# A spline evaluated on two engines: the far product and one sum move from VectorE and a transfer to GpSimd

## The reference

```python
x_aff = clip(x * a[c] + b[c], -1.5, 1.5)
u = (x_aff + 1.0) * 0.5 * (K - 1)              # K = 32 knots
i = floor(u); t = clip(u - i, 0, 1)
spline = sum(alpha_table[i + n - 1] * basis_n(t) for n in range(4))     # indices clipped, R = 8 columns
y_nl = einsum('bchwr,cr->bchw', spline, mix)
return id_gain[c] * x + y_nl + bias[c]
```

## Time and profile before

| | |
|---|---|
| time, median of 3 runs | 1149.39 us (1149.33 to 1150.38) |
| span of the profiled execution | 1143.4 us |
| between the two | 6.0 us, ahead of the first and behind the last instruction |
| PE busy | 1088.0 us, 95% of the span |
| DVE busy | 969.9 us, 85% |
| ACT busy | 898.8 us, 79% |
| POOL busy | 138.8 us, 12% |
| mean granted TensorE clock | 0.991 |

### The profile page before, as it was taken

The page is one execution under the profiler, slowest core; times in us unless marked ns, Lnnn a source line. Parts: engine busy times, 40 slices in busy tenths (PEclk is TensorE's granted clock), DMA queues, the critical chain, the costliest instruction groups (busy, mean ns, idle before and its releaser), DMA issues.

```text
span 1143.4 us, 51639 instructions
## 1 busy us (share of the span) xinstructions
PE 1088.0 (95%) x23882; PEld 726.6 (64%) x23882; DVE 969.9 (85%) x959; ACT 898.8 (79%) x410; POOL 138.8 (12%) x195
## 2 busy tenths in 40 slices
PE   6999999699999959999999999999999999999996
PEld 5777777577777735666666656565665666566564
DVE  4856656687767679999999999999998999999997
ACT  4445453766777548999999999999999999999971
POOL 6000000068100000110101101011010110110100
PEclk9999999899999989999999999999999999999999
DMA  8677674677676937799999999989999989999652
GB/s 278 227 293 283 251 283 175 220 257 301 248 296 270 373 137 173 183 235 232 221 228 218 222 236 216 224 201 236 226 214 231 218 217 235 219 226 209 150 127 86
DMA packets 57459, 259.37 MB, mean 227 GB/s; under 512 B 16080, under 2 KB 16080, under 8 KB 49232
## 3 DMA queue, kind: packets, MB, share of 16 engines
q1 hardware_dynamic: 48496, 208.40, 56.0%
q0 software_dynamic: 8640, 48.17, 23.1%
q10 hardware_dynamic: 160, 0.30, 0.1%
HBM read 104.29 MB, written 77.07 MB: 159 GB/s over the span
## 4 chain that ended last, share of the span: by engine, by line
PE 86%; DVE 7%; issue 3%; DMA 1%; ACT 1%; SPq 0%; ACTq 0%; DVEq 0%
PE tab L1302 48%; PE acc L741 30%; PE tab L1311 7%; DMA halo<-y_scratch 1%; DMA w_raw<-in_w 1%; DVE middle_mask L1160 1%; ACT xin L381 1%; ACT yout L420 1%; DVE far L1187 0%; DVE far_sq L1209 0%; DVE stats L547 0%; DVE lin L1139 0%; DVE offset L1153 0%; DVE edge_mask L1169 0%; DVE poly L1215 0%
## 5 line engine op out<-in xcount | busy, mean ns | idle before, releaser
L1302 PE MATMUL tab<-edge_mask,diag 128*32 128x392 bf16 x10240 | 447.6, 329 | 6.1 <-issue 3.2
L1302 PEld LDWEIGHTS tab<-edge_mask,diag 128*32 128x32 f16 x10240 | 277.0, 97 | 171.0 <-issue 29.4
L1057 ACT ACTIVATE edge_mask<-cell,thr 128x6272 bf16<-128x6272 bf16 x62 | 338.6, 5508 | 1.7 <-DMA cell<-cell 1.7
L420 ACT ACTIVATE yout<-acc 128x1568 f32<-128x1568 f32 x64 | 94.5, 1477 | 167.2 <-PE acc L741 146.3
L741 PE MATMUL acc<-band_split,w 64*64 64x385 f16 (+2 forms) x4608 | 194.8, 329 | 9.8 <-DVE band_split L509 4.5
L741 PE MATMUL acc<-split,w 64*64 64x385 f16 (+3 forms) x4608 | 191.5, 326 | 11.5 <-DVE w L468 10.5
L547 DVE BATCH_NORM_STATS2 stats<-yout 128x392 f32 (+1 forms) x240 | 117.9, 555 | 88.8 <-ACT yout L420 88.8
L1302 PE MATMUL tab<-middle_mask,diag 128*32 128x392 bf16 x4096 | 185.1, 329 | 6.7 <-issue 4.5
L741 PEld LDWEIGHTS acc<-band_split,w 64*64 64x64 f16 x4608 | 148.3, 109 | 56.1 <-issue 8.8
L741 PEld LDWEIGHTS acc<-split,w 64*64 64x64 f16 x4608 | 144.8, 108 | 57.5 <-issue 12.2
L1302 PEld LDWEIGHTS tab<-middle_mask,diag 128*32 128x32 f16 x4096 | 109.2, 97 | 70.3 <-issue 7.7
(11 more groups left out here) (140 smaller groups left out, 961.6 us busy)
## 6 DMA issues: line engine op xcount, KB each, us to landing
y_scratch<-yout SPq DMA_DIRECT2D x32, 1568.0 KB, 6.1
cell<-cell SPq DMA_DIRECT2D x496, 98.0 KB, 5.1
xin<-y_scratch SPq DMA_DIRECT2D x16, 1568.0 KB, 6.2
lin<-far POOLq DMA_DIRECT2D x32, 784.0 KB, 9.4
out<-lin SPq DMA_DIRECT2D x31, 784.0 KB, 5.8
xin<-in_x SPq DMA_DIRECT2D x15, 1568.0 KB, 6.8
lin<-y_scratch SPq DMA_DIRECT2D x30, 784.0 KB, 9.3
lin<-in_x POOLq DMA_DIRECT2D x28, 784.0 KB, 8.1
```

Of the source, the lines that this page charges most:

```text
L420: act.activation(yout[b][:, :].rearrange("p (r k x) -> p k r x", r=2, k=TILES)[:, 2 * part:2 * part + 2], acc[:, 4 * part:4 * part + 4, 0: ...
L1057: act.activation(mask_of(c, q)[:, :, :], cell4[c % 2][:, :, :], ACT.Sign, bias=thr[:, q:q + 1]).then_inc(sign_mask_ready, 1)
L1302: mm = pe.matmul(tab[(c + t) % 2][j * GROUP:(j + 1) * GROUP, sub, 0:SUB], keep["diag"][part][:, j % 2, t, q, :], mask_of(c, q)[:, j, sub * ...
```

## The change

VectorE's `far_part` and GpSimd's `add_far` go. GpSimd gets two tensor operations per chunk instead, each over 128 x 1568 fp32 elements with two SBUF inputs: `far_part` (`far` times `far_sq`, without the amplitude) and `add_terms` (`far` plus `poly`). VectorE's `slope` writes in place over `offset`, read as fp32 (`sloped`). `slope_and_far` takes the place of `add_slope` and adds the far product to the slope term, in `far`. `value` then adds the value term to `far`. GpSimd's `add_terms` adds the square term, which is left in `poly`, and `finish` multiplies this sum by the amplitude and adds it to `lin`. `finish` now waits for `add_terms`, and `slope_and_far` for GpSimd's `far_part`. For the last chunk VectorE makes the sum itself (`last_terms`).

```diff
         copied = [sem(f"cell_copied{b}") for b in range(2)]
         stored = [sem(f"out_stored{b}") for b in range(LIN)]
         x_added = sem("x_added")
-        far_added = sem("far_part_added")
         scaled = sem("scaled")
         sum_ready = sem("sum_ready")
         sum_half = sem("first_half_sum_ready")
...
         table_used = sem("table_used")
         far_part_ready = sem("far_part_ready")
         dist_sq_ready = sem("dist_sq_ready")
-        slope_ready = sem("slope_ready")
+        slope_ready = sem("slope_and_far_ready")
+        terms_added = sem("terms_added")
         whole = sem("chunk_whole")
         block = keep["block"]
...
         def used(c, t):
             return TABLES * c + t + 1
+
+        def sloped(c):
+
+            return offset[c % 2][:, :].bitcast(F32)
         def image_half(t, c):
             return t[c // 2][:, (c % 2) * CHUNK:(c % 2 + 1) * CHUNK]
...
                 pool.wait_ge(scaled, c - AHEAD + 1)
                 pool.dma_start(lin_of(c)[:, :], image_half(x, c), accum_op=ALU.add).then_inc(x_added, 16)
-            def add_far(c):
-
-                pool.wait_ge(far_part_ready, c + 1)
-                pool.dma_start(lin_of(c)[:, :], far[c % 2][:, :], accum_op=ALU.add).then_inc(far_added, 16)
+            def far_part(c):
+
+                pool.wait_ge(table_used, used(c, T_FAR))
+                pool.wait_ge(far_sq_ready, c + 1)
+                pool.tensor_tensor(far[c % 2][:, :], far[c % 2][:, :], far_sq[:, :],
+                                   ALU.mult).then_inc(far_part_ready, 1)
+
+            def add_terms(c):
+
+                pool.wait_ge(table_used, used(c, T_VAL))
+                pool.tensor_tensor(far[c % 2][:, :], far[c % 2][:, :], poly[c % 2][:, :],
+                                   ALU.add).then_inc(terms_added, 1)
             for c in range(CHUNKS):
                 if AHEAD <= c + 3 < CHUNKS:
                     add_x(c + 3)
-                add_far(c)
+                far_part(c)
+                if c < CHUNKS - 1:
+                    add_terms(c)
         @block.scalar
         def _(act):
...
             def distance(c):
                 act.wait_ge(offset_ready, c + 1)
+                wait_past(act, terms_added, c - 1)
+                act.activation(poly[c % 2][:, :], offset[c % 2][:, :], ACT.Abs, scale=1 / POINT).then_inc(dist_ready, 1)
+
+            def far_distance(c):
+
+                act.wait_ge(dist_ready, c + 1)
                 wait_past(act, whole, c - 1)
-                act.activation(poly[c % 2][:, :], offset[c % 2][:, :], ACT.Abs, scale=1 / POINT).then_inc(dist_ready, 1)
-
-            def far_distance(c):
-
-                act.wait_ge(dist_ready, c + 1)
-                wait_past(act, far_added, 16 * (c - 1))
                 act.activation(far[c % 2][:, :], poly[c % 2][:, :], ACT.Relu, bias=cc(MINUS_1)).then_inc(far_ready, 1)
             def far_square(c):
                 act.wait_ge(far_ready, c + 1)
-                wait_past(act, slope_ready, c)
+                wait_past(act, far_part_ready, c)
                 act.activation(far_sq[:, :], far[c % 2][:, :], ACT.Square).then_inc(far_sq_ready, 1)
             def distance_square(c):
...
                 dve.scalar_tensor_tensor(out=quarters(far[c % 2]), in0=summed(c, T_FAR), scalar=base(c, T_FAR),
                                          in1=quarters(far[c % 2]), op0=ALU.add, op1=ALU.mult).then_inc(table_used, 1)
-            def far_part(c):
-
-                dve.wait_ge(table_used, used(c, T_FAR))
-                dve.wait_ge(lin_ready, c + 1)
-                dve.scalar_tensor_tensor(out=far[c % 2][:, :], in0=far[c % 2][:, :], scalar=cc(AMP), in1=far_sq[:, :],
-                                         op0=ALU.mult, op1=ALU.mult).then_inc(far_part_ready, 1)
-
             def square(c):
                 dve.wait_ge(dist_sq_ready, c + 1)
...
             def slope(c):
+                dve.wait_ge(dist_ready, c + 1)
+                dve.wait_ge(dist_sq_ready, c + 1)
+                dve.wait_ge(table_ready, used(c, T_LIN))
+                dve.scalar_tensor_tensor(out=quarters(sloped(c)), in0=summed(c, T_LIN), scalar=base(c, T_LIN),
+                                         in1=quarters(offset[c % 2]), op0=ALU.add, op1=ALU.mult).then_inc(table_used, 1)
+
+            def slope_and_far(c):
+
+                dve.wait_ge(table_used, used(c, T_LIN))
                 dve.wait_ge(far_part_ready, c + 1)
-                dve.wait_ge(table_ready, used(c, T_LIN))
-                dve.scalar_tensor_tensor(out=quarters(far_sq), in0=summed(c, T_LIN), scalar=base(c, T_LIN),
-                                         in1=quarters(offset[c % 2]), op0=ALU.add, op1=ALU.mult).then_inc(table_used, 1)
-
-            def add_slope(c):
-
-                dve.wait_ge(table_used, used(c, T_LIN))
-                dve.scalar_tensor_tensor(out=poly[c % 2][:, :], in0=far_sq[:, :], scalar=1 / POINT,
-                                         in1=poly[c % 2][:, :], op0=ALU.mult, op1=ALU.add).then_inc(slope_ready, 1)
+                dve.scalar_tensor_tensor(out=far[c % 2][:, :], in0=sloped(c), scalar=1 / POINT,
+                                         in1=far[c % 2][:, :], op0=ALU.mult, op1=ALU.add).then_inc(slope_ready, 1)
             def value(c):
                 dve.wait_ge(slope_ready, c + 1)
                 dve.wait_ge(table_ready, used(c, T_VAL))
-                dve.scalar_tensor_tensor(out=quarters(poly[c % 2]), in0=summed(c, T_VAL), scalar=base(c, T_VAL),
-                                         in1=quarters(poly[c % 2]), op0=ALU.add, op1=ALU.add).then_inc(table_used, 1)
+                dve.scalar_tensor_tensor(out=quarters(far[c % 2]), in0=summed(c, T_VAL), scalar=base(c, T_VAL),
+                                         in1=quarters(far[c % 2]), op0=ALU.add, op1=ALU.add).then_inc(table_used, 1)
             def finish(c):
-                dve.wait_ge(table_used, used(c, T_VAL))
-                dve.wait_ge(far_added, 16 * (c + 1))
-                dve.scalar_tensor_tensor(out=lin_of(c)[:, :], in0=poly[c % 2][:, :], scalar=cc(AMP),
+                dve.wait_ge(terms_added, c + 1)
+                dve.wait_ge(lin_ready, c + 1)
+                dve.scalar_tensor_tensor(out=lin_of(c)[:, :], in0=far[c % 2][:, :], scalar=cc(AMP),
                                          in1=lin_of(c)[:, :], op0=ALU.mult, op1=ALU.add).then_inc(whole, 1)
-            def closing_quarters():
+            def last_terms():
                 c = CHUNKS - 1
                 dve.wait_ge(slope_ready, CHUNKS)
-                dve.wait_ge(far_added, 16 * CHUNKS)
+                dve.wait_ge(table_used, used(c, T_SQ))
+                dve.tensor_tensor(poly[c % 2][:, :], poly[c % 2][:, :], far[c % 2][:, :],
+                                  ALU.add).then_inc(terms_added, 1)
+
+            def closing_quarters():
+
+                c = CHUNKS - 1
+                dve.wait_ge(terms_added, CHUNKS)
+                dve.wait_ge(lin_ready, CHUNKS)
                 for sub in range(4):
                     own = slice(sub * SUB, (sub + 1) * SUB)
                     dve.wait_ge(table_ready, used(c, T_VAL) + sub)
...
             total(3)
             far_cube(0)
             linear(0)
-            far_part(0)
             middle(1, MIDDLE_QUADS[0])
             square(0)
             offsets(1)
             slope(0)
             middle(1, MIDDLE_QUADS[1])
-            add_slope(0)
+            slope_and_far(0)
             value(0)
             linear(1)
             linear(2)
...
                 near_cube(c)
                 finish(c - 1)
                 far_cube(c)
-                far_part(c)
                 if c + 1 < CHUNKS:
                     middle(c + 1, MIDDLE_QUADS[0])
                 square(c)
...
                 slope(c)
                 if c + 1 < CHUNKS:
                     middle(c + 1, MIDDLE_QUADS[1])
-                add_slope(c)
+                slope_and_far(c)
+            last_terms()
             closing_quarters()
         @block.tensor
```

More of the change, by code:

```diff
@@ L1030, in distance @@
                 act.wait_ge(offset_ready, c + 1)
-                wait_past(act, whole, c - 1)
+                wait_past(act, terms_added, c - 1)
                 act.activation(poly[c % 2][:, :], offset[c % 2][:, :], ACT.Abs, scale=1 / POINT).then_inc(dist_ready, 1)
@@ L1036, in far_distance @@
                 act.wait_ge(dist_ready, c + 1)
-                wait_past(act, far_added, 16 * (c - 1))
+                wait_past(act, whole, c - 1)
                 act.activation(far[c % 2][:, :], poly[c % 2][:, :], ACT.Relu, bias=cc(MINUS_1)).then_inc(far_ready, 1)
@@ L1221, in value @@
                 dve.wait_ge(table_ready, used(c, T_VAL))
-                dve.scalar_tensor_tensor(out=quarters(poly[c % 2]), in0=summed(c, T_VAL), scalar=base(c, T_VAL),
-                                         in1=quarters(poly[c % 2]), op0=ALU.add, op1=ALU.add).then_inc(table_used, 1)
```

(18 more changed lines are left out.)

## The result

The changed kernel takes 1199.16 us (median; 1197.56 to 1200.41), against 1149.89 us for the kernel before in the same rounds: a ratio of 1.042, 95% interval 1.039 to 1.045. The change is a loss of about 50 us. The forecast was 1186 us and slower, with a range of 1147 to 1206 and, for its likeliest case, 1168 to 1206.

The account below looks back on a forecast made before the run. PE bounds the kernel before at 21.99 us a chunk, DVE the changed one at 23.03. Span 1143.4 plus 28 (27 chunks), 4 (first two), 1.85 (end), with 6.0 around it and 3 for signals: 1186 us, range 1147 to 1206.

Parts of the forecast that it names:

- DVE becomes the bound: Per chunk, DVE's 19.15 us of work plus both stalls gives 23.03 us, above PE's 21.99.
- The two engines exclude each other, both ways and for a whole operation: POOL operations and DVE's `fixed`, `linear`, `offsets`, `middle` block each other; faint sign: a small DVE step 46 ns longer.
- The price of an operation: Each POOL tensor operation of 1568 elements takes 3.55 us, range 3.3 to 3.85.
- The second stall, at `finish`: `add_terms` on POOL starts behind `linear`, so DVE's `finish` waits 1.97 us for it each chunk.
- the rival given 0.07: POOL gets in between `fixed` and `linear`; `linear` stands 3.65 us, `finish` not: 24.7 us a chunk, 1229 us; chance 0.07.
- The first stall, at `offsets`: POOL's `far_part` starts behind the first `middle` and runs beside `square`; DVE's `offsets` then stands for 1.91 us.
- The sum: 19.15 us of DVE work plus stalls of 1.91 and 1.97 makes 23.03 us a chunk; 1186 us in all.
- The 3 us for signal delays at the hand-overs: Two hand-overs from POOL each chunk, 0.05 us each, would add 3 us in all.
- The end: After the last chunk, `last_terms` adds a two-tensor step on DVE, 1.85 us.
- What the transfers are worth: Removing the `add_far` transfers might close PE's gaps, 0.47 us a chunk; priced at 0, at most 12.7 us.
- The rival that had the gaps closing: DVE is not held by POOL, and PE's gaps close as the transfers go: 1137 us; chance 0.06.
- The moved issue of `add_x`: POOL issues `add_x` behind `add_terms`, some 6 us later; the transfer stays hidden by 2 us, costing nothing.

Follow-up runs that it names:

- e6: Changed kernel with GpSimd's two operations replaced by same-size ones on a private buffer nobody waits for; far product and square term missing: 1155.66 us, ratio 1.009.
- e9: As e6, with 784 elements instead of 1568 in both GpSimd operations: 1135.11 us, ratio 0.990.
- e5: Kernel before without its accumulating transfer, so the far part is missing from the result: 1136.24 us, ratio 0.991.
- e10: Changed kernel with GpSimd's addition given to VectorE and `offsets` moved ahead of the first `middle`: 1210.99 us, ratio 1.054.

## Why the prediction was right, and where a step of it was wrong

**DVE becomes the bound: right.** A chunk went from 21.99 to 23.61 us, against 23.03 forecast, and PE waits for DVE. DVE in turn waits 0.55 us a chunk for PE, at `square`, which the sum did not have.

**The two engines exclude each other, both ways and for a whole operation: right.** It was argued from one direction and a faint sign of the other; e6 shows it with operations that nobody needs, and e9 that the hold goes with their length. The Trainium skill's rule (SBUF — State Buffer, SBUF: two separate sides) of an exclusive lock agrees, with a `linear` of 4.32 us for 1.09.

**The price of an operation: right.** 3.50 us, against 3.55 taken. The Trainium skill's figure (GPSIMD Engine Reference, Performance versus the Vector engine), in proportion an estimate of 3.44 us, lay as near.

**The second stall, at `finish`: wrong in place and size.** The prediction said that `fixed` and `linear` follow back to back and that POOL gets in behind `linear`, for a stall of 1.97 us at `finish`. POOL got in between them, and `linear` stood for 3.23 us; `finish` did not wait. This is the mechanism of the rival given 0.07. It had been set aside because at 239.30 a POOL operation waited through two DVE instructions back to back. That row was no accident: POOL waited through the pair all five times that one met its short operations, between 238.9 and 289.3, for 3.32 to 3.35 us. But those two read two SBUF tensors each, and `fixed` and `linear` read one; and the POOL operation there was another, of 32 elements and one tensor. So the row was of another kind. Why POOL loses to the one pair and wins against the other, no run here settles.

**The first stall, at `offsets`: right in kind, too large.** Forecast 1.91 us. Measured are 0.95 of hold and some 0.6 by which `square` came later, waiting for PE, while POOL ran on. The wait for PE, which the sum had dropped, covers part of a hold. The prediction looked for a hole ahead of `offsets`; the profile has no hole there, but an `offsets` recorded as busy for longer.

**The sum.** The chunk came out 0.58 us above the forecast, 15.7 us over 27 chunks, out of three errors. The second stall was 1.26 us longer than forecast (3.23 against 1.97). The first was 0.34 shorter (0.95 and 0.62 against 1.91). DVE's work without stalls was 0.33 shorter: 23.62 less 3.23, 0.95 and 0.62 leaves 18.82, where the sum took 19.15. That the last two go against the first is luck, and so it is partly luck that the time lies in the range: the prediction had priced the mechanism that came about at 1229 us. That rival's 24.7 us a chunk was too long by the same first stall and the same 19.15, and by a `linear` held for 3.65 us instead of 3.23. The 3 us for signal delays at the hand-overs have no row to show them: `slope_and_far` and `finish` follow the step before them without a hole. Taking the 6.0 us for time around the span raised the forecast by some 4 us, which brought it nearer to the measured time: against the span the miss is 18 us (1180 forecast), against the time 13.

**The end: right.** `last_terms` costs 1.8 us (1.85 forecast).

**What the transfers are worth: wrong.** The prediction took 0 for PE's gaps, since no row named a transfer beside them, and kept 12.7 us for the range. e5 measures some 11 us, 7 to 13 by its interval. In the changed kernel, which has no `add_far` transfers either, PE's waits from 480 to 1060 us name DVE alone, 37.6 us in all. By this view the gain was there, but hidden behind the waits for DVE. The rival that had the gaps closing was right about the gaps, and wrong that they would show.

**The moved issue of `add_x`: right.** It comes later in the chunk and nothing waits for it.

## What to carry to other kernels

Work moved from VectorE to GpSimd has to be placed by what VectorE does in the next microseconds, not by VectorE's busy share: beside steps that read PSUM it was free here, and in front of a step with one SBUF input it cost up to its whole length. Look for the hold in instructions that became longer, not in idle time. Where a change loses, test what its parts would be worth without the collision before dropping it: here 11 us stood behind the loss, and moving two steps brought 0.8% over the kernel before.

## What was not expected of the hardware

A waiting GpSimd operation gets in between two VectorE steps of one SBUF input each that follow back to back: in front of `linear` (4.32 us) in the changed kernel and of `middle` (5.12 us) there, once, and in e10. Against two steps of two SBUF inputs each it waited through both (3.32 us). The held step is recorded as busy, not as waiting.

An accumulating transfer of 784 KB per chunk costs about 0.4 us a chunk in a stage that TensorE bounds: 21.99 us a chunk with it, 21.58 without, and 6.4 us of waits in TensorE's own queue between 480 and 1060 us with it, 0.2 without.

An operation of GpSimd that reads the same buffer twice was 0.74 us shorter than one that reads two (3.58 against 4.32 us, each with its wait for VectorE). That buffer also held only zeros, and no run tells the two reasons apart.
